# A decoder block with eight routed experts: separate lists for first and second choices, and expert rows added onto the stored residual by accumulating indirect transfers

## The reference, cut to what matters

```
x = x + linear_attention(layernorm(x))                 # 16 heads, causal, 128 sequences of 64 tokens, D = 128
x = x + cross_attention(layernorm(x), ctx, ctx, mask)  # 16 heads
xf = layernorm(x)                                      # 8192 tokens
probs = softmax((layernorm(xf) * ln_scale + ln_bias) @ gate_w.T)      # 8 experts
p2, i2 = top_k(probs, 2);  w = p2 / (sum(p2) + EPS)
out = swiglu(xf, sWg, sWu, sWd)                        # the shared expert, 128 -> 256 -> 128
for e in range(8):
    out = out + w[:, e:e+1] * swiglu(xf, Wg[e], Wu[e], Wd[e])
return x + out
```

## Time and profile before

| | |
|---|---|
| runs, us | 939.54, 942.29, 942.96 (median 942.29) |
| profiled execution, us | 942.9 |
| its span, from the first to the last instruction | 941.1 |
| mean granted TensorE clock | 0.95 of full speed |
| busy share of the span | PE 87%, PEld 73%, DVE 73%, ACT 66%, POOL 62% |
| chain that ended last | PE 44%, DVE 34%, ACT 8%, issue 7%, DMA 3%, POOL 2%, SPq 2% |

### The profile page before, as it was taken

One profiled execution on the slowest core, in us unless ns is written; L12 is line 12 of the kernel. 1 busy time (PEld: TensorE's weight loads), 2 busy tenths in 40 slices (PEclk: granted clock), 3 DMA queues, 4 the chain that ended last, 5 costly groups with the idle time before them and its releaser, 6 DMA issues.

```text
span 941.1 us, 26449 instructions
## 1 busy us (share of the span) xinstructions
PE 816.2 (87%) x9293; PEld 683.3 (73%) x9293; DVE 688.9 (73%) x1900; ACT 617.2 (66%) x1228; POOL 581.5 (62%) x657
## 2 busy tenths in 40 slices
PE   4789999989999999999999986898989999999900
PEld 3567788777777777777777765687879898989800
DVE  2236677988988988988978897667757777777645
ACT  3567797797788788788787665553336666666600
POOL 5356365877877867967966776424716666665710
PEclk9799999999999999999999988899999999999955
DMA  9101111021022021021021200501103333333289
GB/s 247 37 19 29 47 47 47 25 58 58 24 58 58 25 61 55 24 64 55 23 65 54 64 26 24 157 16 50 40 23 92 89 89 93 91 88 87 70 237 298
DMA packets 92413, 66.25 MB, mean 70 GB/s; under 512 B 8943, under 2 KB 84472, under 8 KB 92288
## 3 DMA queue, kind: packets, MB, share of 16 engines
q1 hardware_dynamic: 75424, 43.46, 17.1%
q0 software_dynamic: 8416, 16.93, 5.4%
q10 hardware_dynamic: 8448, 4.20, 1.5%
HBM read 42.44 MB, written 22.56 MB: 69 GB/s over the span
## 4 chain that ended last, share of the span: by engine, by line
PE 44%; DVE 34%; ACT 8%; issue 7%; DMA 3%; POOL 2%; SPq 2%; POOLq 0%; ACTq 0%; DVEq 0%
PE pair_x L778 7%; PE bank L796 6%; DVE mx L1309 6%; DVE Ex L1313 5%; PE pair_y L778 3%; DVE c_t L1374 3%; PE bank L533 2%; PE bank L695 2%; DMA Kblk<-mixed 2%; PE pair_y L683 2%; PE pair_x L683 2%; PE bank L455 2%; PE pair_x L608 2%; PE pair_x L514 2%; PE bank L764 2%
## 5 line engine op out<-in xcount | busy, mean ns | idle before, releaser
L1215 POOL DMA_INDIRECT mixed<-f_y,f_x x135 | 131.3, 973 | 89.8 <-issue 61.4
L1137 POOL DMA_INDIRECT routed<-c_row,c_idx x128 | 136.9, 1069 | 40.7 <-issue 40.7
L1094 POOL TENSOR_TENSOR Qblk<-qT,con 128x512 f32<-128x512 f32 x64 | 66.9, 1051 | 63.8 <-DVE qT L1269 63.5
L796 PEld LDWEIGHTS bank<-Qblk,Am 128*128 128x128 f32 x540 | 79.5, 190 | 13.5 <-issue 2.3
L625 PEld LDWEIGHTS bank<-Cblk,ExT 128*64 128x64 f32 x2048 | 65.7, 139 | 27.3 <-issue 18.1
L1309 DVE TENSOR_REDUCE mx<-pair_y 128x16 f32<-128x1024 f32 x64 | 78.1, 1220 | 9.8 <-PE pair_y L594 8.9
L608 PE MATMUL pair_x<-con,Ex 128*128 128x128 f32 x512 | 70.4, 281 | 14.3 <-ACT Am L892 11.8
L796 PE MATMUL bank<-Qblk,Am 128*128 x540 | 82.2, 275 | 0.2 <-DVE Am L1562 0.2
L608 PEld LDWEIGHTS pair_x<-con,Ex 128*128 128x128 f32 x512 | 56.2, 143 | 34.6 <-issue 31.6
L929 ACT COPY ExT<-pair_x 128x1024 f32<-128x1024 f32 x64 | 64.4, 1006 | 25.7 <-PE pair_x L608 25.3
L1313 DVE TENSOR_TENSOR Ex<-pair_y,mx 128x1024 f32<-128x1024 f32 x64 | 78.4, 1225 | 2.2
(11 more groups left out here) (212 smaller groups left out, 2223.9 us busy)
## 6 DMA issues: line engine op xcount, KB each, us to landing
f_x<-routed SPq DMA_DIRECT2D x135, 65.0 KB, 1.9
ctxD<-in_ctx SPq DMA_DIRECT2D x32, 256.0 KB, 4.0
ctxP<-in_ctx SPq DMA_DIRECT2D x16, 256.0 KB, 2.9
maskB<-in_mask_BxS_if SPq DMA_DIRECT2D x16, 256.0 KB, 4.1
Cblk<-mixed SPq DMA_DIRECT2D x16, 256.0 KB, 5.6
Kblk<-mixed SPq DMA_DIRECT2D x16, 256.0 KB, 6.0
block_out<-X ACTq DMA_DIRECT2D x16, 256.0 KB, 5.8
mixed<-f_y,f_x POOLq DMA_INDIRECT x135, 2.3
```

The lines of the kernel that those rows point to most:

```text
L796: ins = pe.matmul(banks[F_O[n % 2]][:, 0:D], f_hT[:, u % 3, c * P:(c + 1) * P], wdn[:, bass.ds(e, 1), c, :].rearrange("p o d -> p (o d)"), ...
L1094: return pool.tensor_tensor(dst[:, j, :, :, :], both.to_broadcast([P, 2, RH, T]), rows, ALU.mult)
L1137: pool.indirect_dma_start(routed[:, :], bass.IndirectOffsetOnAxis(ap=c_idx[:, par, t, n:n + 1], axis=0), c_row[:, par, t, n, :], None, bou ...
L1215: pool.indirect_dma_start(mixed[:, :], bass.IndirectOffsetOnAxis(ap=f_x[:, u, D + 1:D + 2].bitcast(I32), axis=0), f_y[:, u, :], None, boun ...
```

## The change: two lists of experts, and sums made by the transfer

First choices and second choices get lists of their own, each with eight expert regions, in `routed` (now 2 x `PHASE_ROWS` rows). A list needs at most `PHASE = (8192 + 8*127) // 128 = 71` tiles, so 142 tiles are run. Within one list each token occurs once. Before the routed tiles, SP stores all of `X`, shared expert included, to the output. POOL then scatters each tile onto the output itself, with `compute_op=ALU.add`: the transfer adds the row of `f_y` to the row that is there. POOL waits for all 16 stores before its first scatter, and for all scatters of the first list before the first of the second. `mixed`, its 32 loads, the 32 additions on DVE and the stores from ACT's queue are gone.

```
-TILE_MAX = (TOP * TOKENS + E * (P - 1)) // P
-SPARE = TILE_MAX - TOP * TOKENS // P
+PHASE = (TOKENS + E * (P - 1)) // P
+TILE_MAX = TOP * PHASE
+SPARE = PHASE - TOKENS // P
+PHASE_ROWS = E * REGION + SPARE * P
...
@@ SP
+            def store(i):
+                sp.wait_ge(S["s_ac"], i + 1)
+                sp.dma_start(tok_out[:, group(i), :], X[:, group(i), :]).then_inc(S["y_st"], 16)
+
+            def pad_lists(n):
+                for e in range(E):
+                    first = n * PHASE_ROWS + e * REGION
+                    at = sp.value_load(t_pad[0:1, n * E + e:n * E + e + 1], min_val=first, max_val=first + TOKENS)
+                    sp.dma_start(routed[bass.ds(at, P), :], pad[:, :]).then_inc(S["t_padded"], 16)
...
+            for i in range(GROUPS // 2):
+                store(i)
             sp.wait_ge(S["t_ch"], 1)
+            pad_lists(0)
             sp.wait_ge(S["t_done"], 1)
...
+            for n in range(UNROLL):
+                load_tile(n)
+            for i in range(GROUPS // 2, GROUPS):
+                store(i)
+            pad_lists(1)
+            for n in range(UNROLL, PHASE):
+                load_tile(n)
+            sp.wait_ge(S["t_padded"], 16 * TOP * E)
+            for n in range(PHASE, TILE_MAX):
+                load_tile(n)
...
@@ PE, c_positions
-                pe.wait_ge(S["c_seld"], d + 1)
+                pe.wait_ge(S["c_ch"], C_STEPS * d + 17)
...
-                pe.matmul(bank[:, 0:GT * E], before[:, :], c_sel[:, :, :].rearrange("p t e -> p (t e)"),
+                pe.matmul(bank[:, 0:n_pos], before[:, :], c_pick[:, :, :, :].rearrange("p n t e -> p (n t e)"),
...
@@ POOL
             def tile_scatter(t, u):
+                if is_first(t, u):
+                    pool.wait_ge(S["y_st"], 16 * GROUPS)
+                if t * UNROLL + u == PHASE:
+                    for w in range(UNROLL):
+                        pool.wait_ge(f_out[w], 16 * turns_of(w, PHASE))
                 pool.wait_ge(S["f_yd"], t * UNROLL + u + 1)
-                pool.indirect_dma_start(mixed[:, :],
+                pool.indirect_dma_start(out_rows[:, :],
...
-                                        f_y[:, u, :], None, bounds_check=TOP * TOKENS - 1, oob_is_err=False)\
+                                        f_y[:, u, :], None, bounds_check=TOKENS - 1, oob_is_err=False,
+                                        compute_op=ALU.add)\
                     .then_inc(f_out[u], 16)
...
@@ DVE
-                dve.tensor_tensor(c_sel[:, :, :], c_pick[:, 0, :, :], c_pick[:, 1, :, :], ALU.add).then_inc(S["c_seld"], 1)
...
-                dve.wait_ge(y_ld[u], 32 * (i // Y_RING + 1))
-                xs = X[:, group(i), :].rearrange("p t d -> p (t d)")
-                dve.tensor_tensor(xs, xs, y_in[:, u * GN:(u + 1) * GN], ALU.add).then_inc(S["y_ad"], 1)
-                dve.wait_ge(S["y_ad"], i + 1)
-                dve.tensor_tensor(xs, xs, y_in2[:, u * GN:(u + 1) * GN], ALU.add).then_inc(S["y_sum"], 1)
```

More of the change, by code:

```diff
@@ L63 @@
 UNROLL = 15
-TURNS = TILE_MAX // UNROLL
 LAG = 6
@@ L71 @@
 SET_ZERO, SET_DVE = 9, 8
-Y_RING = 4
 SB_ALIGN = 32
 CONST = {"ident": P, "late": T, "cos": HALF, "turn": C * HALF, "row": RH, "quarter": C, "half": C, "order": E, "before": P,
-         "region": E, "place": GT * TOP, "upto": E * E, "tile": TILE_MAX}
+         "region": TOP * E, "place": GT * TOP, "upto": E * E, "tile": TILE_MAX, "tile_row": TILE_MAX}
 CONST_AT = dict(zip(CONST, np.cumsum([0, *CONST.values()])[:-1].tolist()))
@@ L99, in shape_constants @@
     part("before")[:] = p[:, None] < p[None, :]
-    part("region")[:] = np.arange(E)[None, :] * REGION
-    n = np.arange(GT * TOP)
-    part("place")[:] = p[:, None] + (n // TOP * P + n % TOP * TOKENS)[None, :]
+    n = np.arange(TOP * E)
+    part("region")[:] = (n // E * PHASE_ROWS + n % E * REGION)[None, :]
+    part("place")[:] = p[:, None] + (np.arange(GT * TOP) // TOP * P)[None, :]
     part("upto")[:] = np.tril(np.ones((E, E))).reshape(1, -1)
-    part("tile")[:] = np.arange(TILE_MAX)[None, :]
+    n = np.arange(TILE_MAX)
+    part("tile")[:] = (n % PHASE)[None, :]
+    part("tile_row")[:] = (n % PHASE + n // PHASE * (PHASE_ROWS // P))[None, :]
     return c
@@ L119, in decoder_block @@
                   consts, out):
-    routed = nc.dram_tensor("routed", [E * REGION + SPARE * P, ROW], F32, kind="Internal").ap()
-    mixed = nc.dram_tensor("mixed", [TOP * TOKENS, D], F32, kind="Internal").ap()
+    routed = nc.dram_tensor("routed", [TOP * PHASE_ROWS, ROW], F32, kind="Internal").ap()
     with ExitStack() as stack:
@@ L217, in decoder_block @@
         c_t = sb("c_t", [P, GT, E])
-        c_pick = sb("c_pick", [P, TOP, GT, E])
-        c_sel = sb("c_sel", [P, GT, E], BF16)
+        c_pick = sb("c_pick", [P, TOP, GT, E], BF16)
         c_m = sb("c_m", [P, GT])
         c_best = sb("c_best", [P, TOP, GT])
-        c_pos = sb("c_pos", [P, GT, E])
+        c_pos = sb("c_pos", [P, TOP, GT, E])
         c_hit = sb("c_hit", [P, TOP, GT, E])
@@ L288, in decoder_block @@
         ctx_p = ctx.rearrange("(t s) k d -> (s k) t d", s=2)
-        mixed_v = mixed.rearrange("(o t p) d -> o p t d", o=TOP, p=P)
+        out_rows = out.rearrange("b k d -> (b k) d")
         def group(i):
@@ L314, in routed_slots, with turns_of @@
         def routed_slots(slot):
[L316 to L320, removed]
+            for n in range(TILE_MAX + LAG):
+                slot(*divmod(n, UNROLL))
         def tile_of(t, u, back):
-            t, u = (t, u - back) if u >= back else (t - 1, u - back + UNROLL)
-            return None if isinstance(t, int) and not 0 <= t < TURNS else (t, u)
+            n = t * UNROLL + u - back
+            return divmod(n, UNROLL) if 0 <= n < TILE_MAX else None
         def is_first(t, u):
-            return isinstance(t, int) and t == 0 and u == 0
+            return t == 0 and u == 0
+        def turns_of(u, tiles):
+            return len(range(u, tiles, UNROLL))
         @block.sync
@@ L358, in _ @@
             sp.wait_ge(S["set_d"], SET_DVE)
-            sp.dma_start(routed[E * REGION:E * REGION + SPARE * P, :].rearrange("(n p) f -> p n f", p=P),
-                         pad[:, :].rearrange("p (o f) -> p o f", o=1).to_broadcast([P, SPARE, ROW]))\
-                .then_inc(S["t_spare"], 16)
+            for n in range(TOP):
+                at = n * PHASE_ROWS + E * REGION
+                sp.dma_start(routed[at:at + SPARE * P, :].rearrange("(n p) f -> p n f", p=P),
+                             pad[:, :].rearrange("p (o f) -> p o f", o=1).to_broadcast([P, SPARE, ROW]))\
+                    .then_inc(S["t_spare"], 16)
             with sp.Fori(1, GROUPS) as j:
@@ L381, in _, with load_tile @@
+            def load_tile(n):
+                t, u = divmod(n, UNROLL)
+                at = sp.value_load(t_row[0:1, n:n + 1], min_val=0, max_val=TOP * PHASE_ROWS - P)
+                if t:
+                    sp.wait_ge(f_out[u], 16 * t)
+                sp.dma_start(f_x[:, u, :], routed[bass.ds(at, P), :]).then_inc(f_in[u], 16)
+            for i in range(GROUPS // 2):
+                store(i)
             sp.wait_ge(S["t_ch"], 1)
-            for e in range(E):
-                at = sp.value_load(t_pad[0:1, e:e + 1], min_val=e * REGION, max_val=e * REGION + TOKENS)
-                sp.dma_start(routed[bass.ds(at, P), :], pad[:, :]).then_inc(S["t_padded"], 16)
+            pad_lists(0)
@@ L385, in _ @@
             sp.wait_ge(S["t_done"], 1)
             sp.wait_ge(S["t_padded"], 16 * E)
-            sp.wait_ge(S["t_spare"], 16)
+            sp.wait_ge(S["t_spare"], 16 * TOP)
             for m in range(2):
                 sp.wait_ge(c_sc[m], 16 * GT * TOP * (GROUPS // 2))
[L392 to L397, removed]
@@ L399, in _ @@
-            for t in range(TURNS):
-                for u in range(UNROLL):
-                    load_tile(t, u)
-            for u in range(UNROLL):
[L405 to L411, removed]
@@ L418, in _ @@
+            for n in range(PHASE, TILE_MAX):
+                load_tile(n)
+            for u in range(UNROLL):
+                sp.wait_ge(f_out[u], 16 * turns_of(u, TILE_MAX))
             sp.wait_ge(S["y_st"], 16 * GROUPS)
@@ L659, in c_positions @@
                     later = GT - 1 - t
-                    pe.matmul(bank[:, (t + 1) * E:GT * E], ones[:, :],
-                              c_sel[:, t:t + 1, :].to_broadcast([P, later, E]), start=False, stop=False,
+                    pe.matmul(pos[:, :, t + 1:GT, :], ones[:, :],
+                              c_pick[:, :, t:t + 1, :].to_broadcast([P, TOP, later, E]), start=False, stop=False,
                               skip_group_check=True)
                 for t in range(GT):
-                    ins = pe.matmul(bank[:, GT * E:(GT + 1) * E], ones[:, :], c_sel[:, t, :], start=False,
-                                    stop=(t == GT - 1), skip_group_check=True)
+                    ins = pe.matmul(bank[:, n_pos:n_pos + TOP * E].rearrange("p (n e) -> p n e", n=TOP), ones[:, :],
```

(20 more changed lines are left out.)

55 lines of the change are left out of this document (24 added, 31 removed).

## The result

| | runs, us | median | ratio to before, 95% interval |
|---|---|---|---|
| before | 939.54, 942.29, 942.96, 943.87, 944.22 | 942.96 | |
| changed | 971.46, 971.80, 972.63, 972.87, 976.90 | 972.63 | 1.0321 [1.0292, 1.0350] |

The profiled execution of the changed kernel took 976.9 us, the longest of its five, with a span of 975.0; sums on its trace are made against that. It also has the lowest mean granted TensorE clock of the five, 0.953 against 0.960 to 0.964 of full speed.

A forecast was written before the change was run, and what follows sets the result against it. PE was taken to bound the routed tiles at 1.464 us each, POOL able to do 1.28. Last landing 898.97, +10.2 for seven tiles, +1.0 landing, +1.8 around the span: 912.0 us, a gain of 30; range 908 to 970.

The forecast's parts named there:

- the accumulating scatter: POOL's scatter with add in the routed tiles: duration taken as 0.97 us, bounds 0.97 and 1.75, up to 1.16 harmless.
- break-even: Scatter duration on POOL at which the gain is gone: 1.37 us, a pace of 1.68 us a tile.
- rival A: Routed tiles: accumulating scatters over 1.16 us make POOL the bound and take back the gain; chance 0.27, nearly all slower.
- the wait between the lists: POOL before tile 71: 0.8 to 2.5 us late, made up in 5 to 14 tiles; 1 to 3 us if POOL bounds.
- rival B: Routed tiles: scatter duration between 1.16 and 1.37 us, time 913 to 942, say 927 at 1.27; chance 0.12.
- rival C: Routed tiles: scatter landings over 9.0 us return the 15 buffers late; break-even at 12 us; chance 0.06, half of it slower.
- The combine's 42.1 us: Behind the last scatter's landing: all loads of mixed, additions and stores go, saving 42.1 us.
- Seven tiles at 1.464: Routed tiles: 142 instead of 135 at PE's pace of 1.464 us, adding 10.2 us that no work hides.
- the add's longer landing: Behind the last tile: the accumulating scatter's landing, 2.1 to 4.3 us, taken as +1.0 us, counted once.
- The first scatter's wait for the stores: POOL's first scatter waits for the stores of X: last lands by 696.1, scatter due at 700.61, cost 0.
- The sign of the main loop's end: A main loop ending more than 2.5 us from 689.9 would show the prediction wrong in any case.
- The DMA engines: Routed tiles: with scatter cost doubled, the stage's DMA share goes from 0.29 to about 0.42; no bound there.

The follow-up runs named there:

- the plain two-list kernel: The changed kernel with the add taken off its scatters, which then overwrite rows of the output: 913.11 us, ratio to before 0.970.

## Why the prediction was wrong

**The step that failed** is the accumulating scatter. I had bounded it between 0.97 and 1.75 us and then took 0.97, "the row of the scatter itself". It measured 1.553. The break-even that the prediction gave was 1.37. With 1.553 the formula of rival A gives 700.6 + 141 x 1.857 + 3.1 + 1.8 = 967.3. It leaves out the wait between the lists (3.3), although the prediction says elsewhere that with POOL as the bound it counts, and it has 3.1 us behind the last scatter's start where the trace has 5.66. With both it gives 973.2, against the median of 972.6; the start 3.6 us later makes 976.8 of it, against 976.9 in the profiled run. So A happened, with its mechanism and its sign, and its formula is 5 us short. What was wrong is its chance of 0.27, and with it the range. The upper end of 970 stood for d = 1.57, above the measured 1.553; it was 2.6 us too low because of the two terms that the formula lacks.

The choice was badly founded in one respect. An instruction that does more than the row it is compared with was priced at the bottom of its bounds, while the point from which it decides lay at the middle. With a margin of 0.19 us for a cost known to within 0.78, the forecast should have been that the time is open, and the range should have reached to the upper bound's 996. The upper bound itself had no good ground: the smallest operation of POOL, 0.195 us, says nothing of the fixed part of a scatter, which is 0.84 us by the runs of 64 and 128 rows. Two sums are off by little, and nothing hangs on them: at d = 1.27 rival B gives 928 and not 927, and the ring of rival C holds 1.464 up to a landing of 8.8 us and not 9.

**What held.** The combine's 42.1 us went as a whole. Seven tiles at 1.464, the two waits, the stores and the pads: the plain two-list kernel has exactly these, and its profiled run is 911.8 against the 912.0 of the sum. That they meet so closely is partly luck, since two small errors cancel: its first scatter came at 698.3 instead of 700.6, and its span ends 4.8 us behind the start of the last scatter, where I had 2.14 + 1.0. In the changed kernel that end is 5.66 us, 0.8 more, and with 64 rows it is 4.6 with the add and 3.6 without, 1.0 more: near the 1.0 that I took for the add's longer landing. With the add on every third tile it is 6.5, which this does not explain.

**The wait between the lists** was 2.0 us with plain scatters, inside my 0.8 to 2.5, and was caught up within 11 tiles, inside my 5 to 14. With the add it was 3.3 us, a little over the 1 to 3 of the prediction, and nothing made it up. What made it longer is the landing of the last scatter of the first list, and SP's load behind that landing shows when it came (timeline of SP, after):

```profile
838.29 0.33 SPq L397 DMA_DIRECT2D f_x<-routed  x1
```

It starts 4.05 us behind the scatter at 834.24; in the plain kernel the same load, at 803.75, is 2.28 us behind the scatter at 801.47. In both kernels POOL's next scatter follows 1.1 us after that load, a part that the prediction did not have: with a landing of 2.3 alone the plain wait would have been 0.8, so that 2.0 lies in my range is luck in part. POOL waits there for 15 semaphores one by one; that this is the 1.1 us was not tried.

**The first scatter's wait for the stores** was hidden: ACT's `f_y` is what ended POOL's idle time at 704.18, not the stores.

**The sign of the main loop's end** (more than 2.5 us from 689.9) was too sharp. The same code ahead of the scatters reached PE's first routed transpose at 693.1 us in the changed kernel's trace and at 687.2 in the plain one's, so what the wider gate costs is lost in the spread of single runs.

**The DMA engines.** I expected their share of the stage to go from 0.29 to 0.42; in the window above it went from 0.33 to 0.52, while fewer tiles passed, and between the first and the last scatter (704 to 969 us) it was 0.49. Rival C stayed out: the longest landing was 4.6 us, with 9 needed.

## What to carry to other kernels

Where an engine stands within 15% of the bound, price each of its instructions that changes before anything else is summed. A new operation on an old instruction is not the old instruction: here 0.58 us more of it, of which POOL had 0.19 to spare, cost 55 us over 141 tiles, more than the 42 of the whole stage that it replaced. With 128 rows of 512 bytes, an accumulating indirect transfer costs nothing if the stage gives POOL 1.86 us for each; below that, what is missing for each transfer has to be set against what the sums cost elsewhere. Work behind the last tile can be shortened without it: split the lists so that all but the last part is combined under the tiles. Here that brought 8 us, of the 29 by which the plain two-list kernel, which leaves out the sums, lies below the kernel before.

## What the runs showed that I had not expected

An indirect transfer costs POOL mostly a fixed price, by the line through 64 and 128 rows: 0.84 us plain and 1.25 with the add, against 1.0 and 2.4 ns a row. The queue rows of the profile (packets, MB, share of 16 engines), before in the earlier trace rows and after here, show what the add does in the transfer itself:

```profile
q0 software_dynamic: 24544, 16.94, 12.4%
```

263 plain transfers made 8416 packets, 32 each. The 128 that stay plain take 4096 of the 24544, so the 142 accumulating ones made 144 each, with the same bytes counted. With 64 rows a plain one still made 32 packets (8640 in all), an accumulating one 80 (15456 in all): in both sizes the add has one packet for each row and 16 more, and the plain transfer the same 32. At 0.193 us of all 16 engines for a plain one, the rest of the share, 0.124 x 975 - 128 x 0.193 = 96 us, is 0.68 us for an accumulating one, 3.5 times as much. The Trainium skill (Collectives: The Full Stack, section "The bandwidth ceiling") names two source reads for each chunk as the reason why a reducing transfer of a collective has half the rate; the factor that this trace shows for indirect rows of 512 bytes is larger, 3.5. None of this was the bound: the DMA engines were at 0.52 in the window above. POOL's price does not go by the packets alone either. With 64 rows the add brings 48 packets and 0.50 us, with 128 rows 112 packets and 0.58 us. What POOL does in the fixed part of 0.41 us no run here shows.
